# A self-attention block on one core: the inverse transposes at the head of the large burst, and the first projection at the head of one of them

## What is computed

```python
h = _group_norm(xf, norm_scale, norm_bias)         # 32 groups, over tokens and channels of a group
qkv = h @ qkv_w + qkv_b                            # 512 -> 1536
...
ch = width // (3 * N_HEADS)                        # 64
q = (q * scale).reshape(bs * N_HEADS, length, ch)
k = (k * scale).reshape(bs * N_HEADS, length, ch)
v = v.reshape(bs * N_HEADS, length, ch)
weight = jnp.einsum('btc,bsc->bts', q, k)
weight = jax.nn.softmax(weight.astype(jnp.float32), axis=-1).astype(qkv.dtype)
a = jnp.einsum('bts,bsc->btc', weight, v)
...
h = h @ proj_w + proj_b
return (xf + h).reshape(b, *spatial, c)
```

## Time and profile before

| | |
|---|---|
| median of 3 runs | 3664.22 us |
| lowest and highest | 3663.39, 3666.87 us |
| the profiled execution | 3661.95 us |
| its span, first to last instruction | 3660.2 us |
| granted TensorE clock, mean share of full speed | 0.992 |
| TensorE matmuls busy | 3439.0 us, 94% |
| VectorE busy | 2790.4 us, 76% |
| ScalarE busy | 2061.7 us, 56% |
| GpSimd busy | 1610.8 us, 44% |
| 16 DMA engines, queue with the moves | 69.7% |

### The profile page before, as it was taken

One profiled execution on the slowest core, in us unless ns is written; L12 is line 12 of the kernel. 1 busy time (PEld: TensorE's weight loads), 2 busy tenths in 40 slices (PEclk: granted clock), 3 DMA queues, 4 the chain that ended last, 5 costly groups with the idle time before them and its releaser, 6 DMA issues.

```text
span 3660.2 us, 67790 instructions
## 1 busy us (share of the span) xinstructions
PE 3439.0 (94%) x24640; PEld 2560.2 (70%) x24640; DVE 2790.4 (76%) x3473; ACT 2061.7 (56%) x3985; POOL 1610.8 (44%) x2762
## 2 busy tenths in 40 slices
PE   5999999999999999999999999999999999999998
PEld 4767777676676767767677677777777767676775
DVE  4778778787787787877777777777778778787776
ACT  4555555565655655556555555655555555555553
POOL 3444444444444444444444444444444444444442
PEclk9999999999999999999999999999999999999999
DMA  3768777677776777767777777777768777677777
GB/s 111 178 164 191 177 176 184 162 194 176 170 193 165 191 171 181 190 166 183 177 180 179 175 186 171 184 177 171 193 162 192 182 176 187 165 191 169 173 183 171
DMA packets 255707, 646.87 MB, mean 177 GB/s; under 512 B 73872, under 2 KB 73872, under 8 KB 255376
## 3 DMA queue, kind: packets, MB, share of 16 engines
q1 hardware_dynamic: 235792, 604.79, 69.7%
q10 hardware_dynamic: 19584, 37.76, 2.9%
HBM read 71.84 MB, written 33.55 MB: 29 GB/s over the span
## 4 chain that ended last, share of the span: by engine, by line
PE 72%; ACT 13%; DVE 6%; POOL 4%; issue 4%; SPq 1%; DMA 0%; POOLq 0%; ACTq 0%; DVEq 0%
PE s_ps L344 16%; PE pv_ps L373 16%; PE c_ps L407 8%; PE c_ps L408 6%; PE c_ps L409 6%; ACT staged L495 6%; ACT probs L475 6%; PE c_ps L419 4%; PE c_ps L421 3%; PE c_ps L420 3%; DVE turned L608 3%; PE c_ps L391 2%; PE c_ps L392 2%; PE c_ps L393 2%; DVE neg_max L625 2%
## 5 line engine op out<-in xcount | busy, mean ns | idle before, releaser
L475 ACT ACTIVATE probs<-s_ps,neg_max 128x1024 f32<-128x1024 f32 x1024 | 1140.6, 1114 | 856.4 <-DVE neg_max L625 854.8
L625 DVE TENSOR_REDUCE neg_max<-s_ps 128x1 f32<-128x1024 f32 x1024 | 1202.8, 1216 | 470.9 <-PE s_ps L344 470.8
L608 DVE STREAM_TRANSPOSE turned<-probs 128x1024 f32<-128x1024 f32 x1024 | 1225.7, 1226 | 297.4 <-ACT probs L475 263.6
L373 PE MATMUL pv_ps<-probs_t,v 128*64 128x256 f32 x8192 | 944.2, 383 | 6.6 <-DMA probs_t<-turned 6.6
L779 POOL COPY inv_wide<-inv_sum 128x256 f32<-128x256 f32 x256 | 101.5, 397 | 1896.1 <-PE pv_ps L355 1888.8
L373 PEld LDWEIGHTS pv_ps<-probs_t,v 128*64 128x64 f32 x8192 | 568.8, 137 | 358.1 <-issue 95.9
L495 ACT ACTIVATE staged<-c_ps,qk_bias 64x256 f32<-64x256 f32 x1024 | 479.3, 468 | 356.1 <-POOL kl L756 254.1
L407 PE MATMUL c_ps<-h_hi,w_hi 128*128 128x256 f32 x2048 | 626.1, 306 | 43.6 <-ACT staged L495 21.5
L409 PE MATMUL c_ps<-h_hi,w_lo 128*128 128x256 f32 x2048 | 586.5, 286 | 0.0
L408 PE MATMUL c_ps<-h_lo,w_hi 128*128 128x256 f32 x2048 | 586.2, 286 | 0.0
L407 PEld LDWEIGHTS c_ps<-h_hi,w_hi 128*128 128x128 f32 x2048 | 397.5, 194 | 144.1 <-issue 77.6
(11 more groups left out here) (71 smaller groups left out, 4877.3 us busy)
## 6 DMA issues: line engine op xcount, KB each, us to landing
probs_t<-turned SPq DMA_DIRECT2D x4096, 128.0 KB, 2.4
x_res<-in_x SPq DMA_DIRECT2D x128, 256.0 KB, 3.0
result<-x_res ACTq DMA_DIRECT2D x128, 256.0 KB, 3.1
x_next<-in_x SPq DMA_DIRECT2D x120, 256.0 KB, 3.4
probs_t<-in_L_conv_qkv_w ACTq DMA_DIRECT2D x4, 768.0 KB, 8.8
turned<-in_x SPq DMA_DIRECT2D x4, 512.0 KB, 12.8
probs_t<-in_L_conv_proj_w ACTq DMA_DIRECT2D x4, 256.0 KB, 13.8
v_bias<-in_L_conv_qkv_b SPq DMA_DIRECT2D x1, 256.0 KB, 16.9
```

Of the source, the lines that this page charges most:

```text
L373: last = nc.tensor.matmul(pv_ps[side][CH * par:CH * (par + 1), 0, :], v_sb[:, ring_of(i, parity), CH * chunk:CH * (chunk + 1)], p_t[:, par ...
L475: nc.scalar.activation(probs[k % 2][:, :], s_ps[k % 2][:, :], ACT.Exp, bias=neg_max[:, k % 4:k % 4 + 1], accum_out=row_sum[:, (k // HALF) ...
L608: nc.vector.transpose(dst, probs[k % 2][:, :].rearrange("p (k b j) -> p k b j", k=CHUNKS, b=QUADS)).then_inc(probs_turned, 1)
L625: nc.vector.tensor_reduce(neg_max[:, k % 4:k % 4 + 1], s_ps[k % 2][:, :], AX.X, ALU.max, negate=True).then_inc(max_ready, 1)
```

## The change

The transposes of the inverse go from the end of every burst to its head, in front of the first unit. In the step of remainder 4 the list becomes projection, first qk unit, second qk unit, and the x transposes stand behind the projection. `SMALL_BEFORE` becomes a table by remainder. The other engines follow: ScalarE copies x first and then stages both qk units, VectorE takes the projection between its two transposes, GpSimd splits the attention first and then both qk tiles. Since `await_bank` goes by the index in the list, the projection now lies in `c_ps0`, the first qk unit in `c_ps1` and the second in the projection's bank.

```diff
--- before.py
+++ after.py
@@ -38,10 +38,10 @@
 GROUP_MEAN_SLOT = 44
 GROUP_VAR_SLOT = 46
 
-LARGE = {0: [("v", 0), ("v", 1)], 4: [("qk", 0), ("proj", 0), ("qk", 1)],
+LARGE = {0: [("v", 0), ("v", 1)], 4: [("proj", 0), ("qk", 0), ("qk", 1)],
          8: [("qk", 2), ("qk", 3), ("qk", 4), ("qk", 5)], 12: [("qk", 6), ("proj", 1), ("qk", 7)]}
 QK_TILES = [0, 1, 4, 5, 2, 3, 6, 7]
-SMALL_BEFORE = 2
+SMALL_BEFORE = {4: 1, 8: 2, 12: 2}
 MOVE_LAG = 4
 SPREAD_LAG = 8
 ATTEND_LAG = 10
@@ -453,12 +453,12 @@
                     scores(b, k)
                     scores(b, k + 1)
                 if k % HALF == 0:
+                    if within(s - SPREAD_LAG, N_SLOTS):
+                        spread_inverse(b, k)
                     for i, (kind, n) in enumerate(LARGE[k % 16]):
-                        if i == SMALL_BEFORE:
+                        if k % 16 in SMALL_BEFORE and i == SMALL_BEFORE[k % 16]:
                             small(b, k)
                         make[kind](b, k, i, n)
-                    if within(s - SPREAD_LAG, N_SLOTS):
-                        spread_inverse(b, k)
                 else:
                     if within(s - ATTEND_LAG, N_SLOTS):
                         attend(b, k)
@@ -548,10 +548,12 @@
                     stage_qk(b, k, 0)
                 if within(s, N_SLOTS):
                     softmax_exp(b, k + 1)
-                if k % 16 == 4 or k % 16 == 12:
+                if k % 16 == 12:
                     stage_qk(b, k, 0)
                 if small_unit(k)[0] == "stats" and within(b + 1, BATCHES):
                     copy_x(b, k)
+                if k % 16 == 4:
+                    stage_qk(b, k, 1)
                 if k % 16 == 4 or k % 16 == 12:
                     stage_qk(b, k, 2)
                 if k % 16 == 8:
@@ -656,11 +658,13 @@
                     turn(b, k)
                 if k % 16 == 0:
                     take_v(b, k, 0)
+                if k % 16 == 4:
+                    take_proj(b, k, 0)
                 if within(s, N_SLOTS):
                     turn(b, k + 1)
                 if k % 16 == 0:
                     take_v(b, k, 1)
-                if k % 16 == 4 or k % 16 == 12:
+                if k % 16 == 12:
                     take_proj(b, k, 1)
                 if k % HALF == HALF - 2 and within(s, N_SLOTS):
                     invert(b, k)
@@ -799,7 +803,7 @@
 
             def four_slots(b, k):
                 m, pair = k % 16, k // 16
-                if m == 4 or m == 12:
+                if m == 12:
                     split_qk(b, k, LARGE[m][0][1])
                 if m == 8:
                     split_qk(b, k, LARGE[m][0][1])
@@ -811,6 +815,8 @@
                     split_h(b, k)
                 if m == 8:
                     add_bias(b, 2 * pair - 1)
+                if m == 4:
+                    split_qk(b, k, LARGE[m][1][1])
                 if m == 4 or m == 12:
                     split_qk(b, k, LARGE[m][2][1])
                 if m == 8:
```

## The result

The changed kernel takes **3426.14 us** (median of 4 runs, 3424.82 to 3426.32). The kernel before took 3663.8 us on the same chip (4 runs, 3662.25 to 3666.87). The ratio is 0.935, with a 95% interval of 0.9333 to 0.9366: 237.7 us less, where 210 were forecast. The time lies inside the range of 3425 to 3505, 1.1 us above its lower bound.

The account below looks back on a forecast made before the run. TensorE, busy 94% of the span, was taken as the bound. Terms of 138 + 36 + 19 + 17 = 210 us off the profiled 3661.95 gave 3452, and 3454 us for the median; range 3425 to 3505.

Parts of the forecast that it names:

- A: Remainder 8: with GpSimd released early, TensorE's stall goes whole, 2.19 us in each of 63 pairs, 138 us.
- D: Slots 44 and 45: the maximum comes earlier, the last qk unit's wait goes, 1.1 us in 15 batches, 17 us.
- B: Remainder 4: the second qk unit no longer waits for its bank behind ScalarE's staging, 36 us together.
- C: Last pair's remainder 2: affine constants ready earlier, 14.3 us, plus 4.7 us of waits for `h_lo`, 19 us.
- changeovers: TensorE's switches between kinds of matmul in 256 bursts: taken as 0, with 26 us possible either way.
- The rest of the statistics' delay stays: Slots 44 and 45: delay from the batch statistics beyond the 1.1 us taken as gain remains; no size given.
- `kl` gone: Sign at ScalarE: its 254.1 us of waits for `kl` disappear, replaced by waits for qk units.
- Rival 1: Attend steps: VectorE sets the pace, each loses 0.2 us, 51 us come back, 3505 us; chance 12%.
- Rival 2: Remainder 8: ScalarE's q stagings still late, half of A stays, 69 us, 3523 us; chance 8%.
- Rival 3: Burst head: the inverse waits for VectorE's scaling of attention, 2.1 us per burst, slower at 3983 us; chance 2%.
- Rival 4: Shared port: a general lock makes GpSimd's and VectorE's busy times follow each other, 4401 us; chance 1%.
- Rival 5: Widening: GpSimd is not freed, since it also waits for VectorE's reciprocal, 3664 us; chance 1%.

Follow-up runs that it names:

- Head in remainder 8 only: The kernel before with the inverse at the head in the bursts of remainder 8 alone, old list order: 3489.85 us, ratio 0.952.
- tail in remainder 8 only: The changed kernel with the inverse back at the end in the bursts of remainder 8 alone: 3602.71 us, ratio 0.9828.
- the two buffers: The kernel before, inverse at the tail, with two buffers `inv_wide` for GpSimd's widening and the projection's bias left out: 3461.72 us, ratio 0.9443.
- order only: The changed kernel with the inverse back at the end of every burst, leaving the new list order of remainder 4: 3627.85 us, ratio 0.9896.
- head only: The kernel before with the inverse at the head of every burst, the order of remainder 4 unchanged: 3439.63 us, ratio 0.9384.
- the two buffers in the changed kernel: The changed kernel with two buffers `inv_wide` as well, the projection's bias left out: 3425.67 us, ratio 0.934.

## Why the prediction was right, and what it missed

**The mechanism stands.** Head in remainder 8 only and tail in remainder 8 only agree from both sides on A and D together (10.20 and 10.03 us per batch, where the table has 9.16 + 1.07), the two buffers show that the blocked GpSimd queue is the cause, and order only separates B. By terms, from the table of steps, per batch of four pairs:

| term | forecast per batch | measured | from which steps |
|---|---|---|---|
| A | 4 x 2.19 = 8.76 | 9.16 | remainder 10: 4 x 1.80; remainder 12: 0.48, 0.48, 0.40, 0.60 |
| B | 3 x 0.33 + 1.15 = 2.14 | 2.06 | remainder 4: 0.26, 0.26, 0.25, and 1.29 in the last pair |
| C | 0.95 + 4.7 / 15 = 1.26 | 1.24 | last pair: remainder 2 0.53, remainder 4 0.40 and 0.31 for `h_lo` |
| D | 1.10 | 1.07 | slot 44: 1.47, less A's 0.40 |
| changeovers | 0 | 0.50 | the other steps |
| sum | 13.26 | 14.03 | |

In the last pair's remainder 4 the 2.00 us are split by the forecast's own shares for C, and slot 44's 1.47 by its share for A; the steps alone don't tell these apart. Order only shortens the first by 0.98 and head only by 1.50 us: which of the two is credited with the 0.48 us that either brings is a matter of choice, so 1.29 for B is not a measurement of B alone.

**A.** Right, and the working with it: the q staging starts at S + 6.37 (forecast 6.8), the exponential is 0.26 us late (0.2), the attend loses nothing. The forecast counted 0.40 us for the slower scores behind the stall; step 12 shortened by 0.48 and, in the last pair, by 0.60. With the head in remainder 8 only, which leaves the inverse of step 12 at the tail, it shortened by 0.42 and 0.56; the 0.05 between is changeover.

**B.** Right: VectorE's addition ends the wait in time. It starts at 1698.26 for 0.69 us, and the second qk unit at 1699.49. ScalarE's stagings are late, as forecast, without cost:

```profile
1698.26 0.69 DVE L648 TENSOR_TENSOR x_res<-c_ps,x_res 128x512 f32<-128x512 f32 x1
...
1699.70 3.86 ACT L495 ACTIVATE staged<-c_ps,qk_bias 64x256 f32<-64x256 f32 x8 [1.65 <-PE c_ps L409]
1703.58 1.11 ACT L475 ACTIVATE probs<-s_ps,neg_max 128x1024 f32<-128x1024 f32 x1
```

They end at 1703.56 = S + 10.13 with S = 1693.43; the forecast had 10.3. Head only shows what the prediction did not say: about half of these waits go with the inverse, without the new order. Order only shows the reverse: VectorE's addition is in time in the last pair only because the head has removed the delays in front of it.

**C and D.** Right in size. For D the maximum of slot 44 starts 2.81 us after its scores (1668.97 against 1666.16), where 2.95 was forecast. "The rest of the statistics' delay stays" holds as well, 0.44 us of it in front of the last unit:

```profile
1668.97 2.29 DVE L627 TENSOR_REDUCE neg_max<-s_ps 128x1 f32<-128x1024 f32 x2
...
1672.39 0.47 ACT L490 ACTIVATE staged<-c_ps,qk_bias 128x256 f32<-128x256 f32 x1
...
1672.91 0.39 PE L407 MATMUL c_ps<-h_hi,w_hi 128*128 128x256 f32 x1 [0.44 <-ACT staged L490]
```

**What was missed, 26 us.** The sum of 210 against the 235.7 us between the spans. Three parts:
- 10.4 us are a term that the prediction lacked: TensorE's clock, 8.9 us in the middle batches and 1.5 in the first. It is told below. Another 1.4 us are the smaller pieces of the account above.
- In the 14 middle batches the forecast's four terms make 14 x 13.26 = 185.6 us, the steps 196.4: some 11 us more. Of these, 14 x 0.50 = 7.0 us are the term "changeovers", which the prediction took as 0 between bounds of 26 us either way, and 14 x 0.40 = 5.6 us are A's, mostly the scores behind its stall and the changeover in step 12; B, C and D give back 1.8.
- The remaining 3 us lie in the first and the last batch and were not taken apart.

That the time is still inside the range is in part luck. Its lower bound was meant for changeovers that gain and D going whole; the result comes within 1.1 us of it, less than the 7 us that a measurement tells from none, and 10.4 us of the way there are the clock, which no bound had counted.

**What would show it.** TensorE busy 98%: as forecast. Its idle time fell by 152 us, where the prediction had about 160 of the gain in it, and its busy time by 83 us, where it had 50 for slower matmuls. A pair without statistics 52.35 us: forecast 52.5. `kl` gone: yes. GpSimd's wait for the inverse "some 600": 810.0. That number was too low; that the wait is free is shown by the two buffers in the changed kernel. TensorE's waits for exponentials: the matmuls of L344 wait 6.2 us in 5 times, none of them in an ordinary pair of the batch shown; the 57.6 us in 133 waits of the weight load (204.7 before) lie under the attend's last matmuls, whose hand-over is 3.60 us. Idle time in front of the inverse: the matmuls show 0.0, the weight load 91.9 us of "issue", at most 0.6 each, beside running matmuls.

**The rivals.** Rival 1 (VectorE's pace): refuted by 167 us of added work that cost 19. Rival 2 (ScalarE still late in remainder 8): refuted, no trace of A's stall is left. Rival 3 (the inverse waits for the scaling): the matmul's idle time in front of it is 0.0. Rival 4 (a lock between GpSimd and VectorE): the means of all 1024 maxima and all 1024 transposes, in ns:

```profile
L610 DVE STREAM_TRANSPOSE turned<-probs 128x1024 f32<-128x1024 f32 x1024 | 1233.6, 1229 | 89.9 <-ACT probs L475 70.4 <-DMA probs_t<-turned 0.8
L627 DVE TENSOR_REDUCE neg_max<-s_ps 128x1 f32<-128x1024 f32 x1024 | 1205.3, 1219 | 411.4 <-PE s_ps L344 411.4
```

Before they were 1226 and 1216 ns; 3 ns each is 6 us of VectorE's time in all. By the exemption of the Trainium skill (SBUF — State Buffer, "Who interferes with whom") they should not have changed at all, and to within these 0.2% the trace agrees. The two engines do meet in one place. `dsq`, the square of four numbers per partition, has two inputs, both in SBUF. Before and after the change:

```profile
L697 DVE TENSOR_TENSOR dsq<-dmean 128x4 f32<-128x4 f32 x16 | 2.6, 162 | 0.6
L701 DVE TENSOR_TENSOR dsq<-dmean 128x4 f32<-128x4 f32 x16 | 9.0, 564 | 0.6
```

In 15 of its 16 executions it now takes 0.59 us instead of 0.16. Each time it starts 0.17 us behind GpSimd's `attn_lo`, which also has two SBUF inputs and runs for 0.74 us, and ends 0.02 us behind it. In order only and in head in remainder 8 only, where `attn_lo` comes over 2 us later, `dsq` takes 0.16 us. No step became longer by it: TensorE's waits for `gvar` behind it are 8.2 us before and after. Rival 5 (GpSimd not freed): refuted by 1079 us less waiting.

## What to carry to other kernels

When an engine off the critical path waits long for a single buffer, read what stands behind that wait in its queue, and who waits for that: here 1888.8 us of harmless waiting hid 10 us per batch of harmful waiting two engines on. Such a wait can be moved by issuing the releasing instruction first in its burst, or be removed by a second buffer; one of the two was enough. When a delayed instruction is moved out of a chain, look for the next reader of the same bank: taking the statistics out of the maxima's way gained nothing until the copy that frees the bank had moved too.

## What the runs showed that was not expected

**The clock falls behind a stall.** In the kernel before, some of A's stalls are followed by a stretch at TensorE's lower level. Windows of 1 us in one such place (columns as in the earlier trace rows, the granted clock third from the end):

```profile
605.00:606.00 1.00, 0.00 (x0) 0.00 (x0) 0.00 (x0) 0.97 (x2) 0.92 (x3) 1.00 0.28 105
606.00:607.00 1.00, 0.37 (x4) 0.33 (x6) 0.39 (x1) 1.00 (x3) 1.00 (x2) 1.00 0.00 0
607.00:608.00 1.00, 0.87 (x8) 0.43 (x6) 1.00 (x2) 0.94 (x3) 0.92 (x4) 1.00 0.00 0
608.00:609.00 1.00, 1.00 (x7) 0.55 (x6) 1.00 (x3) 0.00 (x0) 1.00 (x2) 0.77 0.00 0
609.00:610.00 1.00, 1.00 (x6) 1.00 (x6) 1.00 (x2) 0.00 (x0) 0.28 (x1) 0.50 0.00 0
...
612.00:613.00 1.00, 1.00 (x6) 0.83 (x5) 1.00 (x2) 0.89 (x3) 0.00 (x0) 1.00 0.60 127
```

TensorE is idle for the whole of the first microsecond shown and for 0.63 us of the next; from 608 on it is busy throughout, and the clock is granted at 0.50, the 1.2 GHz level, until it is back at 1.00. At that level matmuls of 256 columns follow each other in 0.21 us instead of 0.12:

```profile
609.05 0.41 PE L408 MATMUL c_ps<-h_lo,w_hi 128*128 128x256 f32 x1
609.26 0.41 PE L409 MATMUL c_ps<-h_hi,w_lo 128*128 128x256 f32 x1
```

There are ten such stretches in the 14 middle batches and one in the first, at irregular distances. Each begins 1.3 to 1.9 us behind the end of a stall of A, in which TensorE stood for 1.72 or 2.00 us, and falls on the step of remainder 12. In the first two pairs that step takes 1.5 us longer for it. In the third pair, four times, it costs nothing (0.01 us): the last qk unit then waits 0.06 us for its staging instead of 1.10. The change has none between 120 and 3360 us, nor have head only, head in remainder 8 only and the two buffers; tail in remainder 8 only, which keeps A's stalls, has nine, and order only, which keeps them too, three in its middle batches. So the stretches come with A's stalls, but only with some of them. Why one stall of A is followed by such a stretch and the next one isn't, these runs don't tell. The Trainium skill (TensorE: Matmul & The Clock Gate, Part 1) names the same two levels and ties the lower one to an engine that was idle. The trace agrees on the levels, and in the middle batches the clock fell only behind idle time. Its price here, 10.4 us of 3660, was small but was 4% of the gain.

**The place of the inverse.** At the end of a burst the two transposes put 0.31 us between their start and the next scores (1834.65 to 1834.96); at the head, 0.19 us to the next unit's first matmul (1707.80 to 1707.99). With the ends of the burst counted, the steps of remainder 0 and 8, which nothing else disturbed, became 0.03 to 0.07 us shorter (medians over the 14 middle batches). With the inverse still at the tail, in order only, they stayed within 0.02 us of what they were. No matmul was saved; the order alone did this.
